# One change to a state-space and expert block: a quarter of the scans' inputs are made by ScalarE and TensorE

## The chip, the cores and the metric

The kernel runs on one NeuronCore of one Trainium2 chip. Its engines are TensorE (PE in the profile, its weight loads PEld), VectorE (DVE), ScalarE (ACT), GpSimd (POOL) and SyncE (SP, which here only issues DMAs). The metric is the time of one execution on the device in microseconds.

## The reference, cut to what matters

All data is float32. For x of shape (2, 1024, 256):

```
h  = x @ (W_base + 2 * sum_e cond[e] * B_e A_e)^T + b       # one weight per batch entry
x += mamba(h) forward + flip(mamba(flip(h)))                # two directions
x += ffn(cond2(x))                                          # 8 experts, 2 per token

mamba(h):                       # 512 channels d, 16 states n, time t
  xs, z = in_proj(h);  xs = silu(causal_conv4(xs) + cb)
  dt_r, B, C = x_proj(xs);      dt = softplus(dt_r @ W + b)
  s[d,n,t] = exp(dt[d,t] * A[d,n]) * s[d,n,t-1] + (dt[d,t] * xs[d,t]) * B[n,t]
  y[d,t]   = sum_n C[n,t] * s[d,n,t] + D[d] * xs[d,t];   out = (y * silu(z)) @ out_proj
```

The change is about the term (dt * xs) * B, the input product of a state's scan.

## The kernel before

The scans are cut into 256 units of 2 blocks of 128 channels, one state and 512 times. The four passes q (two batch entries, each forward and backward) have 64 units each: two halves of time, in each two pairs of blocks, in each the 16 states. So a group of 16 units shares its dt and its dt times x, and unit number i modulo 16 is the state. Channels lie on partitions and time along the row. The blocks of a pair are called j = 0 and j = 1.

For each unit the engines do this, every one in its own written order, held together by semaphores:

- ScalarE, `decay(i)` (L762): exp(dt * A) for both blocks. Block 1 goes into one of two PSUM banks (`DE`), block 0 into a ring of three in SBUF (`dA`). It waits until the scans two and three units before have ended.
- VectorE, `u(i)` (L964): block 0's input product, from the bank `DU` (dt times x) and a row of B, into the bank `U`. Then `scans(i)` (L974): a scan for block 1 (L988), which reads `DE` and GpSimd's product, and a scan for block 0 (L991), which reads `dA` and `U`. Results go into `hh`, a ring of three. In units 3, 7, 11, ... (every fourth, `OWN`) block 0's result stays in `U` and VectorE itself multiplies it by C (`own_product`, L994).
- GpSimd, `u(turn)` (L1218): block 1's input product for two units at a time, into `uA`. `product(i)` (L1232): the states times C for both blocks (L1245), or for block 1 alone in own units (L1241), into `hc`, a ring of four.
- TensorE, `add(i)` (L467): adds the products into two PSUM banks `Y`, as eight 128x128 transposes, so that the sum stands turned; in the last 32 units as plain products with the identity. At a group's start `turn_back`, ScalarE's copies (L801, L807) and `first_sum` (L448, D times x with a diagonal as one operand) come between. TensorE runs two units behind (`LAG`).
- SyncE, `ring_load(turn)` (L1339): the rows of B and C for two units, spread over all partitions, from DRAM into a ring of three slots, as two DMAs. A slot's load waits for GpSimd's and VectorE's last product from it.

At a group's start VectorE makes dt times x for block 0 (`du`, L954), after ScalarE has copied dt into `DU` (L778), and GpSimd for block 1 (`du`, L1209).

Beside this runs side work, placed in slots by tables at the head of the file (`STEP_AT`, `CONV_SLOTS`, `XD_AT`, `GATE_AT`, `TILE_AT` and others): the next pass's projections, convolution, step widths (softplus as Relu, Exp and Ln, added by a DMA that GpSimd issues, L1258), gates, output projection and tiles. TensorE does a unit's side work ahead of its `add`. The convolution multiplies by diagonals that ScalarE makes from the identity (`conv_diag`, L702), as it does for D (L783). Ahead of the scans stands a short stage that makes the weights and the first pass's inputs; behind them come routing and 39 expert tiles, which the change doesn't touch.

## Time and profile before

| | us |
|---|---|
| median of 3 runs | 1394.02 |
| lowest, highest | 1393.07, 1407.0 |
| the profiled execution | 1399.34 |
| its span in the trace | 1397.5 |
| the stage of the scans, in the trace | from 40 to 917 |

The profile is one execution, seen by the hardware's own recorder: every instruction with start, duration, line and what released it. Busy time counts an engine's instructions without their overlap. A wait is the engine's idle time before an instruction, put down to what ended last. Start times within an engine can be closer than the durations, since neighbouring instructions overlap by about 0.1 us. The granted clock is a share of TensorE's 2.4 GHz, and is 1.0 or 0.5 at any moment.

### The profile page before, as it was taken

The page shows a single profiled execution, that of the slowest core. Times are in us where ns is not written, and L with a number is a line of the kernel's source. Part 1 is how long each engine was busy: PE and PEld are TensorE (multiplying, and loading weights), DVE is VectorE, ACT ScalarE, POOL GpSimd, SP SyncE. Part 2 cuts the span into 40 slices and gives each one's busy share as a digit, 9 for nine tenths or more (in the row PEclk, how much of TensorE's full clock was granted, in tenths as well). Part 3 has the DMA queues.
Part 4 walks back from the last instruction along what each step waited for, and adds up shares of the span by engine and source line. Part 5 has one row for each costly group of instructions (what it writes and reads, how often), then busy time and mean ns, then how long its engine had stood idle before and what let it go on. Part 6 is the DMA issues. An engine that isn't in the chain of part 4 may idle for free.

```text
span 1397.5 us, 19024 instructions
## 1 busy us (share of the span) xinstructions
PE 1193.3 (85%) x6488; PEld 882.5 (63%) x6488; DVE 939.3 (67%) x1140; ACT 736.6 (53%) x1324; POOL 965.0 (69%) x511
## 2 busy tenths in 40 slices
PE   8878878778778768786686778898999999999997
PEld 3455544545445445455465533457999999999996
DVE  3999999999999999999999999962111111111110
ACT  4898776778785677777776574413111111111111
POOL 1999999999999999999999999921222222222211
PEclk9988889998989789798688799988999999999999
DMA  5556455555556464555466553507998999899982
GB/s 202 187 167 182 161 157 165 166 171 174 169 170 181 151 181 152 164 185 163 165 190 190 172 183 135 183 10 266 371 316 307 321 320 318 309 316 320 314 315 46
DMA packets 105507, 290.55 MB, mean 208 GB/s; under 512 B 9649, under 2 KB 19506, under 8 KB 89922
## 3 DMA queue, kind: packets, MB, share of 16 engines
q1 hardware_dynamic: 95762, 271.24, 56.0%
q0 software_dynamic: 9648, 18.09, 6.5%
q8 instruction: 52, 0.85, 0.2%
q14 instruction: 45, 0.37, 0.1%
HBM read 271.47 MB, written 9.96 MB: 201 GB/s over the span
## 4 chain that ended last, share of the span: by engine, by line
DMA 40%; PE 35%; POOL 17%; issue 3%; SPq 3%; DVE 1%; POOLq 0%; ACT 0%; DVEq 0%; ACTq 0%
DMA arena<-bc_scratch 39%; POOL arena L1245 10%; PE ps_y L653 10%; PE ps L664 9%; PE ps_u L653 5%; PE ps_du L653 5%; POOL arena L1241 4%; SPq L1349 3%; POOL arena L1229 2%; PE ps_y L368 1%; PE ps_y L442 1%; DVE arena L946 1%; PE ps_de L639 1%; PE ps_de L627 1%; DMA arena<-in_xT 0%
## 5 line engine op out<-in xcount | busy, mean ns | idle before, releaser
L1245 POOL TENSOR_TENSOR arena<-arena 128x1024 f32<-128x1024 f32 x192 | 456.6, 2404 | 16.0 <-DVE arena L991 14.3
L444 PE MATMUL ps_y<-ident,arena 128*128 128x128 f32 x1840 | 277.6, 303 | 137.1 <-POOL arena L1245 132.9
L444 PEld LDWEIGHTS ps_y<-ident,arena 128*128 128x128 f32 x1840 | 234.9, 156 | 244.8 <-POOL arena L1245 181.6
L1229 POOL TENSOR_TENSOR arena<-arena 128x1024 f32<-128x1024 f32 x127 | 303.7, 2391 | 8.4 <-issue 4.8
L773 ACT ACTIVATE ps_de<-arena,An 128x512 f32<-128x512 f32 x256 | 176.2, 688 | 203.5 <-DVE arena L988 202.6
L1294 POOL DMA_INDIRECT out_x<-arena x39 | 61.8, 1584 | 305.2 <-ACT arena L926 191.9
L972 DVE TENSOR_TENSOR ps_u<-ps_du,arena 128x512 f32<-128x512 f32 x256 | 178.7, 698 | 23.9 <-DVE arena L1002 8.6
L1196 DVE TENSOR_TENSOR arena<-ps_du,arena 128x512 f32<-128x512 f32 x39 | 27.0, 691 | 230.8 <-PE ps_du L653 227.7
L773 ACT ACTIVATE arena<-arena,An 128x512 f32<-128x512 f32 x256 | 181.3, 708 | 0.0
L988 DVE TENSOR_TENSOR_SCAN arena<-ps_de,hlast,arena 128x512 f32<-128x512 f32 x128 | 163.1, 1274 | 3.5 <-ACT arena L773 1.9
L988 DVE TENSOR_TENSOR_SCAN arena<-ps_de,arena 128x512 f32<-128x512 f32 x128 | 155.3, 1213 | 3.7 <-ACT arena L773 3.2
L653 PE MATMUL ps_y<-arena 128*128 128x128 f32 x1248 | 152.2, 275 | 2.2 <-issue 1.8
L653 PEld LDWEIGHTS ps_y<-arena 128*128 128x128 f32 x1248 | 148.4, 192 | 4.6 <-issue 1.9
L664 PE MATMUL ps<-arena 128*128 128x256 f32 x624 | 141.2, 379 | 0.5 <-issue 0.5
L664 PEld LDWEIGHTS ps<-arena 128*128 128x128 f32 x624 | 115.6, 190 | 15.0 <-issue 0.9
L991 DVE TENSOR_TENSOR_SCAN arena<-arena,hlast,ps_u 128x512 f32<-128x512 f32 x96 | 120.5, 1255 | 0.0
L350 PE MATMUL ps<-arena 128*128 128x512 f32 x224 | 114.5, 636 | 0.4 <-ACT arena L691 0.4
L991 DVE TENSOR_TENSOR_SCAN arena<-arena,ps_u 128x512 f32<-128x512 f32 x96 | 114.7, 1194 | 0.0
L926 ACT ACTIVATE arena<-ps 128x256 f32<-128x256 f32 x39 | 14.9, 383 | 180.4 <-PE ps L664 157.1
L1196 DVE TENSOR_TENSOR arena<-ps_u,arena 128x512 f32<-128x512 f32 x39 | 27.0, 691 | 120.7 <-PE ps_u L653 120.7
L920 ACT ACTIVATE arena<-ps_y 128x512 f32<-128x512 f32 x78 | 46.6, 597 | 114.0 <-PE ps_y L653 112.6
L1241 POOL TENSOR_TENSOR arena<-arena 128x512 f32<-128x512 f32 x64 | 85.0, 1328 | 0.2 <-DVE arena L988 0.2
(228 smaller groups left out, 1667.1 us busy)
## 6 DMA issues: line engine op xcount, KB each, us to landing
arena<-bc_scratch SPq DMA_DIRECT2D x256, 512.0 KB, 4.7
arena<-in_W SPq DMA_DIRECT2D x117, 1024.0 KB
arena<-arena POOLq DMA_DIRECT2D x15, 512.0 KB, 5.0
arena<-in_xT SPq DMA_DIRECT2D x2, 1024.0 KB, 6.4
arena<-in_w2c SPq DMA_DIRECT2D x1, 2048.0 KB, 8.6
arena<-in_xT SPq DMA_DIRECT2D x4, 512.0 KB, 6.1
X_scratch<-stg SPq DMA_DIRECT2D x12, 128.0 KB, 4.6
out_x<-stg SPq DMA_DIRECT2D x12, 128.0 KB, 5.0
```

Source lines behind the costliest of these rows:

```text
L350: t = e.matmul(PS[p][:, :], cdiag[:, m % 2, k, :], xp[:, m, f:f + 512], start=(k == 0), stop=(k == KC - 1))
L444: t = e.matmul(Y[j][:, part], src[:, part], ident[:, :], start=False, stop=stop, is_transpose=True, skip_group_check=True)
L653: t = e.matmul(PS[o][:, j * 128:j * 128 + 128], w[:, i % NW, k, f:f + 128], xsT[:, i % 2, k, :], start=(k == 0), stop=(k == 1))
L664: t = e.matmul(PS[7][:, 0:C], hT[:, i % 2, k, :], w2[:, i % NW, k, :], start=(k == 0), stop=(k == 7))
L773: t = e.activation(DE[i % 2][:, :] if j else dA[:, i % ND, :], dt[:, width_at(q, th, m), :], ACT.Exp, scale=An[:, q % 2, m, n:n + 1])
L972: e.tensor_tensor(U[:, :], DU[:, :], ring[:, turn % NR, 0, i % 2, :], ALU.mult).then_inc(dv_u, 1)
L988: e.tensor_tensor_scan(hh[:, i % NH, 1, :], DE[i % 2][:, :], uA[:, i // 2 % 2, i % 2, :], hlast[:, 2 * pr + 1, n:n + 1] if th else 0.0, AL ...
L991: e.tensor_tensor_scan(U[:, :] if own(i) else hh[:, i % NH, 0, :], dA[:, i % ND, :], U[:, :], hlast[:, 2 * pr, n:n + 1] if th else 0.0, AL ...
L1229: e.tensor_tensor(uA[:, turn % 2, :, :], duA.rearrange("p (o t) -> p o t", o=1).to_broadcast([128, 2, TH]), ring[:, turn % NR, 0, :, :], A ...
L1241: e.tensor_tensor(hc[:, i % NP, 1, :], hh[:, i % NH, 1, :], ring[:, turn % NR, 1, i % 2, :], ALU.mult).then_inc(gp_hc, 1)
L1245: e.tensor_tensor(hc[:, i % NP, :, :], hh[:, i % NH, :, :], c, ALU.mult).then_inc(gp_hc, 1)
L1294: e.indirect_dma_start(out, bass.IndirectOffsetOnAxis(dest[:, i:i + 1], 0), yo[:, i % 3, :], None, compute_op=ALU.add).then_inc(l_add, 16)
```

## The change

- Four states of each group, n = 6, 9, 12 and 15, are *turned units*, in all groups but the first: 60 of 256. In these, VectorE and GpSimd make no input product. Instead dt times x is transposed once a group by TensorE (`turn_inputs`) and copied to SBUF by ScalarE (`duT`, time on partitions). B's four rows are transposed likewise (`turn_rows`, `bT`). With time on partitions B[n, t] is one number a partition, so ScalarE multiplies by it with a scaled copy (`u_turned`, four of 128x256 a unit), and TensorE transposes the result back into the banks that the scans read (`u`): block 1 into `DE`, block 0 into `U`. In turned units block 1's decay goes to SBUF.
- GpSimd makes dt times x for both blocks in one instruction of 128x1024, three units ahead of the group; ScalarE copies block 0 into `DU`. In a turn with a turned unit GpSimd's input product has 128x512.
- `dA`, `uA` and `hh` become one ring `hh` of five: decays and inputs are written into it, and the scan overwrites them by the states. `hc` has three places and not four.
- The diagonals of the convolution and of D come from DRAM by SyncE's DMAs (256 KB and 128 KB each) and are no longer made by ScalarE.
- ScalarE loads one table set that holds Exp and Ln ahead of them.

```diff
-NR, ND, NH, NP, KD, LAG, EV, NW = 3, 3, 3, 4, 6, 2, 4, 3
+FLIP, STRIDE = 6, 3
+NR, NH, NP, KD, LAG, EV, NW = 3, 5, 3, 6, 2, 4, 3
...
+def flipped(i):
+    return i >= 16 and i % 16 >= FLIP and (i % 16 - FLIP) % STRIDE == 0
+DU_AT = {16 * g + 1 + j: (g, j) for g in range(1, 16) for j in range(2)}
+ROWS_AT = {max(at(q_, 32 * h_), 16 * (1 - q_ - h_)) + 3: (q_, h_) for q_ in range(NQ) for h_ in range(2)}
...
TensorE
+            def turn_inputs(i):
+                g, j = DU_AT[i]
+                e.wait_ge(gp_du, g + 1)
+                e.wait_ge(dv_sA, i - 1)
+                for part in QUARTERS:
+                    t = e.transpose(DE[i % 2][:, part], duA[:, j, part], ident[:, :])
+                t.then_inc(pe_dT, 1)
...
+            def u(i):
+                e.wait_ge(ac_uT, flips(i))
+                e.wait_ge(dv_sA, i - 1)
+                for k in range(4):
+                    t = e.transpose(DE[i % 2][:, QUARTERS[k]], uT[:, k, 128:256], ident[:, :])
+                t.then_inc(pe_u1, 1)
+                e.wait_ge(dv_sB, i)
+                if own(i - 1):
+                    e.wait_ge(dv_hc, owned(i - 1))
+                for k in range(4):
+                    t = e.transpose(U[:, QUARTERS[k]], uT[:, k, 0:128], ident[:, :])
+                t.then_inc(pe_u0, 1)
             for i in range(NU + LAG):
                 if i < NU:
                     side_work(i)
+                if i + 1 in DU_AT:
+                    turn_inputs(i + 1)
+                if i + 1 in ROWS_AT:
+                    turn_rows(i + 1)
+                if i < NU and flipped(i):
+                    u(i)
                 if i == NU:
                     out_block(1, 0, 1, both_side, (0, 1))
                 if i >= LAG:
                     add(i - LAG)
...
ScalarE
+            def logs_too():
+                if loaded[0] != "logs":
+                    e.preload_act_table_set("natural_log_exp_and_others")
+                    loaded[0] = "logs"
...
+                if i >= NH:
+                    e.wait_ge(dv_sB, i - NH + 1)
+                    e.wait_ge(gp_hc, i - NH + 1)
                 for j in (1, 0):
                     m = 2 * pr + j
-                    if j and i >= 2:
-                        e.wait_ge(dv_sA, i - 1)
-                    if not j and i >= ND:
-                        e.wait_ge(dv_sB, i - ND + 1)
-                    t = e.activation(DE[i % 2][:, :] if j else dA[:, i % ND, :], dt[:, width_at(q, th, m), :], ACT.Exp,
-                                     scale=An[:, q % 2, m, n:n + 1])
+                    to = hh[:, i % NH, j, :]
+                    if j and not flipped(i):
+                        if i >= 2:
+                            e.wait_ge(dv_sA, i - 1)
+                        to = DE[i % 2][:, :]
+                    t = e.activation(to, dt[:, width_at(q, th, m), :], ACT.Exp, scale=An[:, q % 2, m, n:n + 1])
...
+            def u_turned(i, ks):
+                q, th, pr, n = unit(i)
+                if flips(i) > 1:
+                    e.wait_ge(pe_u0, flips(i) - 1)
+                f = (n - FLIP) // STRIDE
+                for k in ks:
+                    t = e.activation(uT[:, k, :], duT[:, k, :], ACT.Copy, scale=bT[:, q % 2, th, k, f:f + 1])
+                if ks[-1] == 3:
+                    t.then_inc(ac_uT, 1)
...
+                if i + 2 < NU and flipped(i + 2):
+                    u_turned(i + 2, (0, 1))
+                if i + 1 < NU and flipped(i + 1):
+                    u_turned(i + 1, (2, 3))
...
VectorE
             def scans(i):
                 e.wait_ge(ac_dA, i + 1)
+                if flipped(i):
+                    e.wait_ge(pe_u1, flips(i))
...
+                h = hh[:, i % NH, :, :]
+                decay, x = (h[:, 1, :], DE[i % 2][:, :]) if flipped(i) else (DE[i % 2][:, :], h[:, 1, :])
+                e.tensor_tensor_scan(h[:, 1, :], decay, x, hlast[:, 2 * pr + 1, n:n + 1] if th else 0.0, ALU.mult,
+                                     ALU.add).then_inc(dv_sA, 1)
+                if flipped(i):
+                    e.wait_ge(pe_u0, flips(i))
+                else:
+                    e.wait_ge(dv_u, plain(i))
...
             for i in range(NU):
-                if i % 16 == 0:
-                    du(i)
-                u(i)
+                if i == 0:
+                    first_du()
+                if not flipped(i):
+                    u(i)
...
GpSimd
+            def du(g):
+                q, th, pr, n = unit(16 * g)
+                k = width_at(q, th, 2 * pr)
+                width_is_whole(e, 8 * q + 4 * th + 2 * pr)
+                for j in range(2):
+                    has_x(e, q, 2 * pr + j, th)
+                e.wait_ge(gp_u, 8 * g)
+                if g >= 2:
+                    e.wait_ge(pe_dT, 2 * (g - 1))
+                    e.wait_ge(ac_dc, g - 1)
+                e.tensor_tensor(duA, dt[:, k:k + 2, :], xc[q % 2][:, 2 * pr:2 * pr + 2, HB[th]], ALU.mult).then_inc(gp_du, 1)
...
             for i in range(NU):
+                if i % 16 == 13 and i + 3 < NU:
+                    du(i // 16 + 1)
...
SyncE
+            def conv_diag(q, m):
+                if m >= 2:
+                    is_full(e, ("cv", q, m - 2, 1))
+                elif q:
+                    is_full(e, ("cv", q - 1, m + 2, 1))
+                e.dma_start(cdiag[:, m % 2, :, :], d["cd"][q % 2, m]).then_inc(l_cd[m % 2], 16)
+            def sum_diag(g):
+                if g:
+                    e.wait_ge(pe_D, 2 * g)
+                e.dma_start(diag[:, :, :], d["dd"][g // 4 % 2, g % 2]).then_inc(l_D, 16)
...
+                elif i % 16 == 8 and i < NU - 16:
+                    sum_diag(i // 16 + 1)
+                if i + 1 in CONV_AT:
+                    q, m, h = CONV_AT[i + 1]
+                    if h == (q == 0) and (q or m >= 2):
+                        conv_diag(q, m)
```

## Rows read from the trace of the kernel before

**Rows 1.** Busy time of each engine from 40 to 917 us, then clock, DMA share, GB/s.
```profile
40.00:917.00 877.00, 692.17 (x3043) 432.81 (x3042) 839.81 (x949) 628.67 (x1100) 852.40 (x415) 0.87 0.53 168
```
**Rows 2.** Groups of VectorE's instructions, 40 to 917 us: busy, mean ns | idle before them.
```profile
L972 DVE TENSOR_TENSOR ps_u<-ps_du,arena 128x512 f32<-128x512 f32 x256 | 178.7, 698 | 23.9 <-DVE arena L1002 8.6 <-issue 0.4
...
L962 DVE TENSOR_TENSOR ps_du<-ps_du,arena 128x512 f32<-128x512 f32 x15 | 10.4, 690 | 0.7 <-ACT ps_du L778 0.7
```
**Rows 3.** VectorE's timeline: start us, duration us, line, shapes, idle before it.
```profile
79.14 0.68 DVE L1002 TENSOR_TENSOR arena<-ps_u,arena 128x512 f32<-128x512 f32 x1
80.02 0.70 DVE L972 TENSOR_TENSOR ps_u<-ps_du,arena 128x512 f32<-128x512 f32 x1 [0.20 <-DVE arena L1002]
80.63 1.21 DVE L988 TENSOR_TENSOR_SCAN arena<-ps_de,arena 128x512 f32<-128x512 f32 x1
81.76 1.20 DVE L991 TENSOR_TENSOR_SCAN arena<-arena,ps_u 128x512 f32<-128x512 f32 x1
83.04 0.70 DVE L972 TENSOR_TENSOR ps_u<-ps_du,arena 128x512 f32<-128x512 f32 x1
...
92.14 0.68 DVE L1002 TENSOR_TENSOR arena<-ps_u,arena 128x512 f32<-128x512 f32 x1
92.73 0.69 DVE L962 TENSOR_TENSOR ps_du<-ps_du,arena 128x512 f32<-128x512 f32 x1
93.46 0.70 DVE L972 TENSOR_TENSOR ps_u<-ps_du,arena 128x512 f32<-128x512 f32 x1
```
**Rows 4.** Groups of GpSimd's instructions, 40 to 917 us.
```profile
L1245 POOL TENSOR_TENSOR arena<-arena 128x1024 f32<-128x1024 f32 x192 | 456.6, 2404 | 16.0 <-DVE arena L991 14.3 <-DMA arena<-bc_scratch 1.4
L1229 POOL TENSOR_TENSOR arena<-arena 128x1024 f32<-128x1024 f32 x127 | 303.7, 2391 | 8.4 <-issue 4.8 <-PE ps_y L444 1.6 <-PE ps_y L442 0.4
...
L1216 POOL TENSOR_TENSOR arena<-arena 128x512 f32<-128x512 f32 x15 | 20.4, 1363 | 0.0
```
**Rows 5.** GpSimd in the timeline, from one input product to the next.
```profile
292.60 2.56 POOL L1229 TENSOR_TENSOR arena<-arena 128x1024 f32<-128x1024 f32 x1
...
298.47 2.52 POOL L1229 TENSOR_TENSOR arena<-arena 128x1024 f32<-128x1024 f32 x1
```
**Rows 6.** Ring loads, 100 to 900 us: issue ns min/median/max, then time to landing.
```profile
L1349 SPq DMA_DIRECT2D arena<-bc_scratch x234: 359/410/1098, 103.3 to 899.3; - x117
...
DMA to landing us min/median/max: 3.4/4.6/6.9
```
**Rows 7.** TensorE in the timeline: eight transposes, half a convolution, eight transposes.
```profile
297.51 1.09 PE L444 MATMUL ps_y<-ident,arena 128*128 128x128 f32 x8 [1.51 <-POOL arena L1245]
298.44 1.88 PE L350 MATMUL ps<-arena 128*128 128x512 f32 x4
...
330.29 1.97 PE L444 MATMUL ps_y<-ident,arena 128*128 128x128 f32 x8 [2.48 <-POOL arena L1245]
```
**Rows 8.** The convolution's matmuls: group with mean ns, and min/median/max ns.
```profile
L350 PE MATMUL ps<-arena 128*128 128x512 f32 x192 | 99.4, 643 | 0.0
...
L350 PE MATMUL ps<-arena x224: 590/592/1062, 69.7 to 608.2; 128*128 128x512 f32 x112
```
**Rows 9.** Groups of ScalarE's instructions, 100 to 900 us.
```profile
L773 ACT ACTIVATE ps_de<-arena,An 128x512 f32<-128x512 f32 x234 | 161.2, 689 | 193.8 <-DVE arena L988 193.0
L773 ACT ACT_TABLE_LOAD x35 | 44.9, 1283 | 0.6
L753 ACT ACT_TABLE_LOAD x14 | 18.0, 1283 | 0.2
L706 ACT ACTIVATE arena<-ident,cw 128x128 f32<-128x128 f32 x48 | 15.2, 387 | 0.0
```
**Rows 10.** The timeline at a group's start: last product, first addition, product of state 3.
```profile
311.50 1.27 POOL L1241 TENSOR_TENSOR arena<-arena 128x512 f32<-128x512 f32 x1
...
320.02 1.04 PE L444 MATMUL ps_y<-ident,arena 128*128 128x128 f32 x8
...
324.33 1.28 POOL L1241 TENSOR_TENSOR arena<-arena 128x512 f32<-128x512 f32 x1
```

## What the change was predicted to do

> **What bounds the kernel now.** I began with the busy shares of the scan stage, the 877 us in which the 256 units run [rows 1]. VectorE and GpSimd are both occupied nearly throughout (839.8 and 852.4 us), ScalarE and TensorE are not (628.7 and 692.2 us). With two engines near full, the busy share doesn't say which one sets the pace, so I read the order of VectorE's instructions next. In its timeline [rows 3] (product is L972, scans L988 and L991, own product L1002, du L962) the starts follow each other at fixed distances: product to first scan 0.61 us, first to second scan 1.13, second scan to next product 1.28, so a plain unit takes 3.02 us; in a unit whose output VectorE multiplies itself, that product and the gap behind it add 0.91. Twelve plain and four own units make some 52.0 us; sixteen such groups, with 0.12 us a unit more where scans start from stored states, du, gates and tiles, fill the stage. Its idle time before the 256 products is 23.9 us in all [rows 2], a tenth of a microsecond each, the gap behind own products and nothing more, and 16 times 52.0, with these additions, leaves no room for waits: **VectorE is the bound**. GpSimd comes next. Its idle time before its two large kinds is 16.0 and 8.4 us [rows 4], 24 us in 877, so it can follow VectorE down by some 3% and no further.
>
> **What VectorE is relieved of.** 60 of its 256 products go (states 6, 9, 12, 15 of 15 groups). 45 of them follow a plain unit: from second scan to the next first scan was 1.28 + 0.61 = 1.89, and becomes the 1.13 of two scans without a dependence: 0.76 each, 34.2 us. 15 (state 12) follow an own product: from its start to the scan was 0.88 + 0.61 = 1.49, and becomes about 0.59, the distance from own product to du [rows 3]: 0.90 each, 13.5 us. Fifteen du's go [rows 2]; each takes 0.69 us, but with it the distance from own product to next product was 1.32 against 0.88 without, so it is worth 0.44 each, 6.6 us. Together **54 us**: 877 becomes 823.
>
> **What GpSimd is relieved of.** In 60 turns the product shrinks from 128x1024 to 128x512, 2.39 to about 1.36 us [rows 4]: 61.8 us less. Its du grows from 1.36 to the 2.39 of a product of that size, 15 times: 15.5 us more. Net 46 us; busy 852.4 becomes 806, and with the 5 us that it idles on issue, 811. So 12 us of room under VectorE are left, half of what it had.
>
> **Ring loads.** Three slots are left as they are, and a load starts when GpSimd ends the last product of the turn three before. Between that and the input product that needs the slot lie one other input product and two state products: in the rows from 292.60 to 298.47, 5.87 us [rows 5]. Where the input product in that gap is a short one and one of the two is an own unit's (twice a group), the gap falls by 1.03 to 4.84 us. The load takes two issues of 0.41 and 4.6 us to land in the median, 6.9 at most [rows 6]: its second half is there after about 5.2. So GpSimd is late by 0.4 (bounds 0 and 1.5), 30 times: 12 us, of which the room of 12 hides most; I put 4 on the path (bounds 0 and 33). The diagonals of conv and D now come by 32 DMAs (6 MB) on SP's queue. Each is put behind a ring load, whose next one comes 5 us later, and their waits are for TensorE work many units old; 256 KB is a quarter of one ring turn. Nothing for these, bound 1 us each where one runs into a ring load, 32 us if all did.
>
> **TensorE's part: the new wait.** A turned unit costs 8 transposes, 1.04 to 1.09 us at full clock and 1.97 at half [rows 7]; with two times four a group for du and a few rounds for B that is 60 + 16 + 1 us, 692 to some 770 of 850. TensorE isn't the bound in the mean, but now VectorE waits for it. The second scan's input can only be turned once the scan before is over: four transposes, some 0.7 us with the signals, under the first scan of 1.13: hidden at full clock, 0.1 late at half. The first scan's input stands in TensorE's queue behind the additions of unit i-3, which wait for GpSimd's product, and behind the side work of unit i. I laid out one group. Let GpSimd start at 0 and never stop (2.34 us for 128x1024, 1.27 for 128x512: the means less the overlap of neighbours): its product 6 ends at 22.5, product 12 starts at 36.9 and ends at 39.3. VectorE's first scans of states 9, 12 and 15 begin 27.5, 36.6 and 44.9 us behind its first one of the group. Product 12 needs both scans of state 12, done 2.4 us behind the start of the first (39.0), so VectorE must have begun 2.1 before GpSimd. That puts the scan of state 9 at 25.4, 2.9 behind product 6, and that of 15 at 42.8, 3.5 behind product 12; for states 6 and 12 it is 3.3 and 3.8. So there are **2.9 to 3.8 us** from the end of product i-3 to the turned unit's first scan. The queue needs 1.1 + 0.7 + signals = 1.9 bare: enough. With a conv half or its like (1.88) it is 3.8: up to 0.9 late. Bare at half clock it is 3.3: up to 0.4 late. With such side work at half clock (3.4) 6.7: 3 to 4 late. By the slots 40 of the 60 have side work in their own unit, some 31 of that size. Conv matmuls take 643 ns in the mean, where 592 is full clock and 1062 the longest [rows 8], so 11% run at half: 3 or 4 units at 3.3, 12 us. At full clock a small lateness counts about once a group, since GpSimd catches up behind it: 15 x 0.4 = 6 us. **18 us** for TensorE; bounds 0 and 60 x 3.5 = 210.
>
> Here the Trainium skill speaks against the change: "TensorE: Matmul & The Clock Gate", Part 4 (PE-mode transpose), says that transposes don't bring the array to its full clock. By that rule more transposes give no clock back and the granted clock stays at the 0.87 of the stage or falls; rounds of eight at 1.04 us in this trace show only that they run at full clock when it is granted. The sum uses the clock as it is.
>
> **ScalarE.** 240 pieces of 128x256 with a scale: between the 0.387 us of 128x128 and the 0.689 of 128x512 [rows 9] lies 0.49, some 0.42 with the overlap of neighbours: 101 us; 30 copies of du, 16. Off go 64 conv and 32 D diagonals at about 0.32, 31 us, and with one table set for Exp and Ln the loads at L753 and as many at L773, 28 x 1.28 = 36 us. Net +50: 629 to 680 of 850. It waited 193 us for VectorE, so this is covered; only where a Silu with its two loads (3.8 us) meets two pieces (0.84) can a decay come late. 3 us; bounds 0 and 20. By the Trainium skill ("ScalarE: Activation LUTs", What ACT_TABLE_LOAD costs) a switch also drains the engine, 2.66 us in all, and 75 us would go; the rows show 0.6 us of idle before 35 loads, so the trace disagrees.
>
> **Rings.** The product ring shrinks from 4 to 3. At a group's start the last product ends at 312.8, the next group's first addition at 321.1, and product 3 starts at 324.3 [rows 10]. That product must now wait for this addition; 3 us are left, at full clock. With du's turns and half clock it fails in a few of 15 groups: 2 us (bounds 0 and 45). In three groups du's early place is 5 us behind the step widths' DMA: 1 us. The common ring of five lets decays run two units further from GpSimd; no gain, since VectorE didn't wait for it.
>
> **The sum.** 54 - 4 - 18 - 3 - 3 = 26 us. The profiled execution took 1399.3 us (span 1397.5), so 1373; the median of the three runs lies 5.3 lower, so **1368 us**.
>
> **Rivals.** (a) *The queue is never late*: leads as laid out hold, GpSimd's late loads lie in its room; VectorE's 54 us all come back: 1340. For it: TensorE idles 185 us in the stage. Against: the two late loads a group follow from plain addition. (b) *The bound passes to GpSimd through the ring*: loads land 1.2 late, 30 times, 36 us less the room of 12, and TensorE's 18: 54 - 24 - 18 - 3 - 3 = 6, or 1388, the change is hidden. For it: landings up to 6.9 us, more traffic. Against: GpSimd waited only 1.4 us for DMA in all. (c) *TensorE's queue becomes a convoy, slower than before*: the place is the first input of a turned unit. From 0.9 us of lateness per turned unit it eats the 54. If the clock is at half in those with side work, 31 x 3.5 + 20 x 0.4 = 116 us are lost: 1394 - 54 + 116 = 1456; with half of them, 1398; I take 1425. For it: TensorE already at 79%, and granted 0.87 only. Against: conv halves ran at full clock in nine cases of ten, and more work fills the gaps. The skill's rule on transposes belongs here and is part of its chance. (d) *It doesn't do what it says*, the table loads stay or a product form is slower: within the other cases' bounds, no case of its own.
>
> **Chances.** Forecast 0.52, (a) 0.15, (b) 0.18, (c) 0.15. What this kernel's measurement can tell is about 1%, 14 us. The forecast's own range, 1350 to 1384, lies nearly all in faster; (b) nearly all in same; (c) holds 0.12 slower and 0.03 same. Faster 0.67, same 0.21, slower 0.12. The range from 1338 to 1402 leaves out the worse part of (c) and the best edge of (a).
>
> **What would show it.** VectorE's product count 196 and its distance scan to scan 1.13 at turned units: step one. GpSimd's 128x1024 input products 67: step two. A VectorE wait on transposes in the first scan, its total (18 us) and whether it stands beside side work: step three. A GpSimd wait for bc_scratch before the product of turns 5 and 7 of a group: the ring. Wrong I would be if GpSimd's wait for VectorE vanished while VectorE waited for GpSimd instead, or if the granted clock of the stage moved by more than 0.05.

## The result: slower by 3.3%

| | before | after |
|---|---|---|
| median, us (4 runs each) | 1397.53 | 1442.62 |
| lowest to highest, us | 1393.07 to 1407.0 | 1437.31 to 1447.99 |
| the profiled execution, its span, us | 1399.34, 1397.5 | 1447.99, 1446.2 |
| the stage of the scans, in the trace | 40 to 917 | 40 to 965 |

The ratio is 1.033, interval [1.029, 1.0369]. 1368 us were predicted, with 1402 as the upper end: the prediction was wrong in sign, and the result lies 18 us beyond the 1425 us of rival (c).

The whole difference is in the scan stage: 925 us for 877, while what follows it takes 481 us in both. The busy time of each engine in that stage, with the columns of [rows 1]:

```profile
40.00:965.00 925.00, 752.74 (x3674) 502.49 (x3673) 794.15 (x874) 674.18 (x1252) 806.52 (x415) 0.90 0.53 166
```

VectorE's busy time fell by 45.7 us and yet the stage grew by 48, so VectorE's idle time grew from 37 to 131. Where it stands is read from the groups of VectorE's instructions (busy, mean ns | idle before them, and what ended most of it), from 40 to 965 us; `arena<-arena,hlast,ps_de` and `arena<-arena,ps_de` are the first scans of the turned units:

```profile
L1054 DVE TENSOR_TENSOR ps_u<-ps_du,arena 128x512 f32<-128x512 f32 x196 | 136.8, 698 | 21.2 <-DVE arena L1086 8.2 <-ACT ps_du L861 1.4 <-issue 0.9
L1069 DVE TENSOR_TENSOR_SCAN arena<-ps_de,hlast,arena 128x512 f32<-128x512 f32 x96 | 122.4, 1275 | 6.1 <-ACT arena L856 6.1
L1069 DVE TENSOR_TENSOR_SCAN arena<-ps_de,arena 128x512 f32<-128x512 f32 x100 | 121.5, 1215 | 15.7 <-ACT arena L856 13.1 <-POOL arena L1331 2.5
...
L1086 DVE TENSOR_TENSOR arena<-ps_u,arena 128x512 f32<-128x512 f32 x64 | 44.0, 688 | 30.2 <-PE ps_y L466 27.8 <-PE ps_y L464 1.6
L1069 DVE TENSOR_TENSOR_SCAN arena<-arena,hlast,ps_de 128x512 f32<-128x512 f32 x32 | 40.8, 1273 | 31.6 <-issue 16.4 <-PE ps_de L611 9.4 <-ACT arena L856 5.8
...
L1069 DVE TENSOR_TENSOR_SCAN arena<-arena,ps_de 128x512 f32<-128x512 f32 x28 | 33.9, 1210 | 21.3 <-PE ps_de L611 21.1
```

The same groups in the kernel before, as far as they are not in [rows 2]:

```profile
L988 DVE TENSOR_TENSOR_SCAN arena<-ps_de,hlast,arena 128x512 f32<-128x512 f32 x128 | 163.1, 1274 | 3.5 <-ACT arena L773 1.9 <-POOL arena L1229 1.4
L988 DVE TENSOR_TENSOR_SCAN arena<-ps_de,arena 128x512 f32<-128x512 f32 x128 | 155.3, 1213 | 3.7 <-ACT arena L773 3.2 <-POOL arena L1229 0.5
...
L1002 DVE TENSOR_TENSOR arena<-ps_u,arena 128x512 f32<-128x512 f32 x64 | 43.9, 687 | 1.1
```

Three waits are new: **52.9 us** before the first scans of the 60 turned units, **29.1 us** more before VectorE's own products (nearly all on the group's first addition), and **14.6 us** more before the other first scans (14.1 of them on ScalarE's decays). Take off 2.7 us less idle before the products and the 45.7 us of work saved: 52.9 + 29.1 + 14.6 - 2.7 - 45.7 = 48.2, the 48 us of the stage. The view puts 16.4 of the 52.9 us down to nothing it shows and 5.8 to ScalarE, but in the timeline 52.7 of them end with TensorE's turn of that input (L611): the scan starts within 0.25 us of its end.

GpSimd, from the same view, is not the one that holds VectorE; it waits for VectorE more than four times as long as before [rows 4]:

```profile
L1347 POOL TENSOR_TENSOR arena<-arena 128x1024 f32<-128x1024 f32 x192 | 456.1, 2387 | 70.6 <-DVE arena L1075 66.6 <-DMA arena<-bc_scratch 2.0 <-PE ps_y L466 1.9
L1331 POOL TENSOR_TENSOR arena<-arena 128x1024 f32<-128x1024 f32 x67 | 160.0, 2389 | 15.5 <-DMA arena<-bc_scratch 15.3
```

**One late turned unit.** The timeline at unit 54 (state 6). TensorE's order is: side work of a unit, the turned input if it has one, then the addition of the unit two back.

```profile
229.57 1.27 POOL L1343 TENSOR_TENSOR arena<-arena 128x512 f32<-128x512 f32 x1
...
230.90 1.92 PE L358 MATMUL ps<-arena,xpT 128*48 128x512 f32 x4
...
232.75 1.09 PE L466 MATMUL ps_y<-ident,arena 128*128 128x128 f32 x8
...
233.77 1.92 PE L358 MATMUL ps<-arena,xpT 128*48 128x512 f32 x4
234.05 1.25 DVE L1075 TENSOR_TENSOR_SCAN arena<-arena,hlast,ps_u 128x512 f32<-128x512 f32 x1
...
235.62 1.09 PE L466 MATMUL ps_y<-ident,arena 128*128 128x128 f32 x8
236.64 1.12 PE L380 MATMUL ps<-arena,dtT 16*128 16x512 f32 x2
...
237.69 0.66 PE L611 MATMUL ps_de<-ident,arena 128*128 128x128 f32 x4
238.19 0.60 PE L617 MATMUL ps_u<-ident,arena 128*128 128x128 f32 x4
238.44 1.28 DVE L1069 TENSOR_TENSOR_SCAN arena<-arena,hlast,ps_de 128x512 f32<-128x512 f32 x1 [3.14 <-issue]
```

VectorE is ready at 235.30. GpSimd's product of unit 51 ended at 230.84, 4.5 us earlier, more than the 2.9 to 3.8 us that I had laid out. But TensorE was by then still at the side work of unit 52 (230.90). Behind it stood the addition of 50, the side work of 53, the addition of 51 and the side work of 54, each running without a gap, and only then the turn, at 237.69. In this stretch it never waited, and ran at full clock: four matmuls of 128x512 in 1.92 us. It was simply two units of side work behind.

Not all late units are like this one. 30 of the 60 turned units wait over 0.3 us, 52.7 us together. I took for each the stretch from the end of GpSimd's product i-3 to the turn. In 18 of them (26.0 us) TensorE had the full clock and no idle time of half a microsecond there. In three (3.3 us) it idled for 0.5 to 1.4 us in the midst of its side work. In nine (23.4 us, all with side work of their own) its granted clock was 0.5 for a part of the stretch or all of it, and in four of the nine it idled too. The longest wait of all, at unit 220, is one of these:

```profile
836.38 2.07 PE L380 MATMUL ps<-arena,dtT 16*128 16x512 f32 x2
838.38 1.12 PE L611 MATMUL ps_de<-ident,arena 128*128 128x128 f32 x4
839.60 1.22 DVE L1069 TENSOR_TENSOR_SCAN arena<-arena,ps_de 128x512 f32<-128x512 f32 x1 [4.56 <-PE ps_de L611]
...
831.90:838.40 6.50, 6.50 (x19) 3.51 (x17) 3.07 (x7) 1.43 (x3) 5.71 (x5) 0.50 0.71 218
```

The last line is the stretch from product i-3 to the turn, with the columns of [rows 1]: TensorE busy all the time, at a granted clock of 0.50. The 51 turned units at full clock wait 29.4 us together, 0.6 each, the nine others 2.6 each.

**One group start.** The changed kernel in the timeline, at unit 160:

```profile
619.91 1.11 PE L596 MATMUL ps_de<-ident,arena 128*128 128x128 f32 x4
...
621.06 0.60 ACT L834 ACTIVATE arena<-ps_de 128x512 f32<-128x512 f32 x1 [3.85 <-PE ps_de L596]
...
623.07 1.28 DVE L1069 TENSOR_TENSOR_SCAN arena<-ps_de,hlast,arena 128x512 f32<-128x512 f32 x1 [2.55 <-ACT arena L856]
...
627.45 1.97 PE L459 MATMUL ps_y<-ident,arena 128*128 128x128 f32 x8 [2.12 <-ACT arena L888]
...
629.25 3.49 PE L483 MATMUL ps_y<-diag,arena 128*128 128x128 f32 x16
...
632.58 1.91 PE L466 MATMUL ps_y<-ident,arena 128*128 128x128 f32 x16
...
633.72 0.69 DVE L1086 TENSOR_TENSOR arena<-ps_u,arena 128x512 f32<-128x512 f32 x1 [4.31 <-PE ps_y L466]
633.78 1.29 POOL L1343 TENSOR_TENSOR arena<-arena 128x512 f32<-128x512 f32 x1 [5.05 <-PE ps_y L466]
...
619.00:631.00 12.00, 9.88 (x36) 6.74 (x35) 7.04 (x7) 6.57 (x12) 9.73 (x5) 0.50 0.49 165
```

ScalarE stands 3.85 us behind TensorE's turn of dt times x, with the decays behind it, so VectorE's scan is 2.55 us late. ScalarE's copies that `turn_back` needs come late too, the group's first addition starts at 632.58, and only it frees the product place that state 3 needs: VectorE's own product waits 4.31 us and GpSimd's 5.05. By the last line TensorE had a granted clock of 0.50 from 619 to 631 us, so this group, the worst of the 15 for the own product, is late by order and by clock together.

### The profile page after: what moved, and what is told of

Same layout as the page of the kernel before. It is cut to its first block and busy times, and to the rows that moved or that the text cites. A ratio compares the mean times of both kernels' runs of the same rounds, so it can differ in the third digit from the quotient of the medians.

```text
span 1446.2 us, 20708 instructions
## 1 busy us (share of the span) xinstructions
PE 1255.5 (87%) x7120; PEld 952.5 (66%) x7120; DVE 895.3 (62%) x1065; ACT 782.6 (54%) x1477; POOL 919.8 (64%) x511
## 5 line engine op out<-in xcount | busy, mean ns | idle before, releaser
L1347 POOL TENSOR_TENSOR arena<-arena 128x1024 f32<-128x1024 f32 x192 | 456.1, 2387 | 70.6 <-DVE arena L1075 66.6
L466 PE MATMUL ps_y<-ident,arena 128*128 128x128 f32 x1840 | 263.1, 294 | 58.3 <-POOL arena L1347 57.8
L466 PEld LDWEIGHTS ps_y<-ident,arena 128*128 128x128 f32 x1840 | 228.1, 152 | 121.9 <-POOL arena L1347 81.9
L856 ACT ACTIVATE arena<-arena,An 128x512 f32<-128x512 f32 x316 | 218.4, 710 | 0.1
L856 ACT ACTIVATE ps_de<-arena,An 128x512 f32<-128x512 f32 x196 | 134.7, 687 | 93.5 <-DVE arena L1069 85.0
L1331 POOL TENSOR_TENSOR arena<-arena 128x1024 f32<-128x1024 f32 x67 | 160.0, 2389 | 15.5 <-DMA arena<-bc_scratch 15.3
L1054 DVE TENSOR_TENSOR ps_u<-ps_du,arena 128x512 f32<-128x512 f32 x196 | 136.8, 698 | 21.2 <-DVE arena L1086 8.2
L869 ACT ACTIVATE arena<-arena 128x256 f32<-128x256 f32 x240 | 108.0, 498 | 61.8 <-PE ps_u L617 61.7
L1069 DVE TENSOR_TENSOR_SCAN arena<-ps_de,arena 128x512 f32<-128x512 f32 x100 | 121.5, 1215 | 15.7 <-ACT arena L856 13.1
L1069 DVE TENSOR_TENSOR_SCAN arena<-ps_de,hlast,arena 128x512 f32<-128x512 f32 x96 | 122.4, 1275 | 6.1 <-ACT arena L856 6.1
```

The costliest lines, as they stand in the source:

```text
L466: t = e.matmul(Y[j][:, part], src[:, part], ident[:, :], start=False, stop=stop, is_transpose=True, skip_group_check=True)
L856: t = e.activation(to, dt[:, width_at(q, th, m), :], ACT.Exp, scale=An[:, q % 2, m, n:n + 1])
L869: t = e.activation(uT[:, k, :], duT[:, k, :], ACT.Copy, scale=bT[:, q % 2, th, k, f:f + 1])
L1054: e.tensor_tensor(U[:, :], DU[:, :], ring[:, turn % NR, 0, i % 2, :], ALU.mult).then_inc(dv_u, 1)
L1069: e.tensor_tensor_scan(h[:, 1, :], decay, x, hlast[:, 2 * pr + 1, n:n + 1] if th else 0.0, ALU.mult, ALU.add).then_inc(dv_sA, 1)
L1331: e.tensor_tensor(to, duA[:, 1:2, :].to_broadcast([128, 2, TH]), ring[:, turn % NR, 0, :, :], ALU.mult).then_inc(gp_u, 1)
```

## The experiments

Ratios are to the kernel before, timed beside it on the same chip, with 95% intervals. "Gained" is against the changed kernel's ratio of 1.033.

**Theory (T):** TensorE's queue is late by its order. A turned unit's input stands behind side work and additions, and every lateness is passed on by ScalarE and the group's first addition. **Rivals:** the third product place (R1), ring and du edits without the turned units (R2), the scaled copies on ScalarE (R3), the amount of TensorE's work, whatever its order (R4).

Rows in this section are of the groups of VectorE's instructions in the scan stage, unless another view is named.

### b_np3: the third product place alone, in the kernel before

```diff
-NR, ND, NH, NP, KD, LAG, EV, NW = 3, 3, 3, 4, 6, 2, 4, 3
+NR, ND, NH, NP, KD, LAG, EV, NW = 3, 3, 3, 3, 6, 2, 4, 3
```

> The kernel before with the product ring hc cut from four places to three, nothing else. Theory A (the small ring is one of the two costs): VectorE's own product of state 3 must now wait for the group's first addition, some 2 us in each of 15 groups, so 20 to 35 us slower than before, about 1422. Theory B (only the turned units cost): the ring hides as I predicted, at most 3 us, about 1397.

1408.19 us, ratio 1.0058 [1.0036, 1.0081]. VectorE's own products wait 14.5 us, 11.3 of them for the first addition:

```profile
L1002 DVE TENSOR_TENSOR arena<-ps_u,arena 128x512 f32<-128x512 f32 x64 | 44.0, 687 | 14.5 <-PE ps_y L444 11.3 <-PE ps_y L442 2.1
```

So the place costs 8 us by itself, between my two expectations (20 to 35, and at most 3), four times the 2 us of my sum, and is no explanation of 45.

### noflip: the change without its turned units

```diff
 def flipped(i):
-    return i >= 16 and i % 16 >= FLIP and (i % 16 - FLIP) % STRIDE == 0
+    return False
-DU_AT = {16 * g + 1 + j: (g, j) for g in range(1, 16) for j in range(2)}
+DU_AT = {}
...
+ROWS_AT = {}
```

> The changed kernel with no turned unit at all: VectorE and GpSimd make all 256 input products, everything else (common ring, three products, diagonals by DMA, GpSimd's double du, one table set) as changed. Theory A: VectorE is relieved of 7 us of du but waits 30 us at state 3: 1410 to 1425. If only turned units cost: 1390. If the new common ring or the DMAs cost too: over 1430.

1404.55 us, ratio 1.0068 [1.004, 1.0097], less than the 1410 to 1425 that I expected. The own products wait longer than in b_np3:

```profile
L1085 DVE TENSOR_TENSOR arena<-ps_u,arena 128x512 f32<-128x512 f32 x64 | 44.0, 687 | 21.6 <-PE ps_y L466 20.1 <-PE ps_y L464 0.5
```

R2 is bounded: ring, wide du, DMA'd diagonals, fewer table loads and the third product place cost 9 us together. That is a net sum: in the profiled execution the scans take from 40 to 929 us, 12 longer than before, VectorE is busy 8.5 us less in them, and idle 20 us more, all of it before the own products. The turned units, which were to bring the gain, cost the other 38 us.

### own2: VectorE's own unit one state earlier

```diff
-OWN = (3, 7, 11, 15, 19, 23, 27, 31)
+OWN = (2, 7, 11, 15, 18, 23, 27, 31)
```

> The changed kernel with the own unit at state 3 moved to state 2, whose product needs an addition of the group before. Theory A: VectorE's wait before its own products (30 us) falls under 5 us and the time by 15 to 30 us, to about 1420; part comes back as waits at the turned units of state 6. Theory B (TensorE is simply overloaded, a wait removed shows up elsewhere): within 8 us of the changed kernel's 1443.

1439.74 us, ratio 1.0294 [1.0258, 1.0331], 5 us gained, as the second of the two expectations had it. The waits before own products are gone, 30.2 to 1.1 us, but those before the turned units' first scans grew by 20, from 53 to 73 us:

```profile
L1086 DVE TENSOR_TENSOR arena<-ps_u,arena 128x512 f32<-128x512 f32 x64 | 43.9, 687 | 1.1
L1069 DVE TENSOR_TENSOR_SCAN arena<-arena,hlast,ps_de 128x512 f32<-128x512 f32 x32 | 40.7, 1273 | 40.3 <-issue 22.6 <-ACT arena L856 8.9 <-PE ps_de L611 8.7
L1069 DVE TENSOR_TENSOR_SCAN arena<-arena,ps_de 128x512 f32<-128x512 f32 x28 | 33.9, 1211 | 32.5 <-PE ps_de L611 31.7 <-ACT arena L856 0.9
```

R1 falls as a cause of its own in the changed kernel: VectorE meets TensorE's backlog at state 3 or at state 6, and a wait that is removed at one comes back at the other.

### early and first: the turned inputs forward in TensorE's order

```diff
-                t.then_inc(pe_u1, 1)
+                t.then_inc(pe_u1, 1)
+
+            def u_second(i):
                 e.wait_ge(dv_sB, i)
...
             for i in range(NU + LAG):
+                if i < NU and flipped(i):
+                    u_second(i)
                 if i < NU:
                     side_work(i)
...
-                if i < NU and flipped(i):
-                    u(i)
+                if i + 1 < NU and flipped(i + 1):
+                    u(i + 1)
```

This is first; in early, `u_second(i)` stands where `u(i)` stood, behind the side work.

> The changed kernel, but TensorE turns the first scan's input a unit earlier, ahead of the additions of unit i-3 and of the side work of unit i; the second input stays behind the side work. Theory A (the first input's place in the queue is the other cost): of the 53 us that VectorE waits before turned units' first scans most goes; 20 to 40 us faster than the changed kernel, about 1412; some waits pass to the second scan. Theory B (TensorE lacks time, not order): within 8 us of 1443.

> The changed kernel with both turned inputs ahead of the unit's side work: the first also ahead of the additions of unit i-3, the second right behind the second scan of unit i-1. The kernel with the first alone moved took 14 us off; between the two kernels with late turns the second took another 20. If both are costs of place in the queue: 30 to 40 us under 1443, about 1408. If TensorE lacks time: above 1420.

early: 1428.83 us, ratio 1.0195 [1.0144, 1.0246]. first: 1423.6 us, ratio 1.0191 [1.0151, 1.0231]. Both gained 19 us by their ratios, so the second step, which took 27 us of waits away, gained nothing that can be told from noise. Both missed what I expected (about 1412 and 1408), and first lies in the range that I had given to TensorE lacking time (above 1420). In early the first scans of the turned units wait 4.7 us instead of 52.9, but their second scans now wait 33, since the second input is still behind the side work. In first, whose rows follow, these waits are 6 us:

```profile
L1079 DVE TENSOR_TENSOR_SCAN arena<-arena,hlast,ps_u 128x512 f32<-128x512 f32 x93 | 117.0, 1258 | 2.9 <-PE ps_u L619 2.8
L1079 DVE TENSOR_TENSOR_SCAN arena<-arena,ps_u 128x512 f32<-128x512 f32 x96 | 114.8, 1196 | 1.7 <-PE ps_u L619 1.7
L1090 DVE TENSOR_TENSOR arena<-ps_u,arena 128x512 f32<-128x512 f32 x63 | 43.3, 688 | 34.1 <-PE ps_y L466 30.1 <-PE ps_y L464 3.2
...
L1079 DVE TENSOR_TENSOR_SCAN ps_u<-arena,ps_u 128x512 f32<-128x512 f32 x32 | 38.6, 1207 | 1.4 <-PE ps_u L619 1.3
L1073 DVE TENSOR_TENSOR_SCAN arena<-arena,hlast,ps_de 128x512 f32<-128x512 f32 x30 | 38.0, 1267 | 4.5 <-ACT arena L860 3.2 <-issue 1.2
L1073 DVE TENSOR_TENSOR_SCAN arena<-arena,ps_de 128x512 f32<-128x512 f32 x28 | 33.7, 1203 | 4.4 <-PE ps_de L611 4.2
```

T holds for the waits, and in time for less than half of the loss: 44 us of waits before first scans went, 6 came up before second scans, and the time fell by 19. The rest of the lateness is now paid at the group start (34.1 us before own products, 34.4 us in all before the plain first scans). And TensorE now stands still ahead of side work and additions: it waits 45.8 us for VectorE before it turns second inputs, where it waited 38.9 in the changed kernel, and 13.7 us for ScalarE's scaled copies, where it waited 0.7.

### late, early_late, first_late, early_late_np: the turns two units later

```diff
-DU_AT = {16 * g + 1 + j: (g, j) for g in range(1, 16) for j in range(2)}
+DU_AT = {16 * g + 3 + j: (g, j) for g in range(1, 16) for j in range(2)}
```

and B's rows two units sooner.

> The changed kernel with the turning of dt times x two units later (states 3 and 4 of the group in place of 1 and 2) and that of B at state 1 in place of 3. Theory A (the group's start costs because ScalarE waits in its own order for TensorE's turns just before it must copy Y): ScalarE's wait for the du transposes (56 us) falls under 35, VectorE's wait before own products (30 us) to about 15, 10 to 20 us faster than the changed kernel, about 1428. Theory B (three product places are the cost, wherever the turns stand): within 6 us of 1443.

> Both edits: the first input turned ahead of the additions, and du turned two units later. Theory A: the savings add up (14 us and 10 to 20), about 1413. Theory B: like the early one alone, 1425 to 1430.

> As the kernel with both edits, and the second input turned ahead of the unit's side work too, so that no turned input stands behind side work. If side work in front is what is left of the queue's cost: the 33 us that VectorE waits before turned units' second scans nearly go, and the time falls by 10 to 25 us more, to about 1395. If TensorE lacks time: the side work, held back by the wait for the second scan, comes late, and nothing or less is gained, 1410 or more.

> As the kernel with both edits, with four product places and four places in the common ring (the same memory) in place of three and five. If the product ring holds back the group's start: the wait before own products goes, 10 to 20 us less than with both edits, about 1398. If it only moves to the turned unit of state 6, as when the own unit was shifted: within 5 us.

All four came out slower than I had expected (1395 to 1428 us), and the fourth product place changed nothing, as its second expectation had it. 1489.43 us, ratio 1.0665 [1.0612, 1.0719], for late; 1.0609 [1.0554, 1.0663] for early_late; 1.047 [1.0409, 1.053] for first_late; 1.0639 [1.0589, 1.0689] with four product places and a ring of four beside it. I had put the turns at a time when I took TensorE for idle; in late's timeline one of the two now stands behind `first_sum` (L483):

```profile
229.14 3.78 PE L483 MATMUL ps_y<-diag,arena 128*128 128x128 f32 x16
...
236.00 0.66 PE L596 MATMUL ps_de<-ident,arena 128*128 128x128 f32 x4
...
236.69 0.60 ACT L834 ACTIVATE arena<-ps_de 128x512 f32<-128x512 f32 x1 [6.74 <-PE ps_de L596]
```

The miss tells more than the hits: the same instructions, at other places in the order, cost 47 us. R4 can't be all: the amount of TensorE's work is the same in both.

### soon, first_soon, first_soon_np: the turns a unit sooner

```diff
-DU_AT = {16 * g + 1 + j: (g, j) for g in range(1, 16) for j in range(2)}
+DU_AT = {16 * g + j: (g, j) for g in range(1, 16) for j in range(2)}
```

B's rows are turned one unit sooner too, and ScalarE's turned copy waits for its own last scaled pieces.

> The changed kernel with the turning of dt times x one unit earlier (states 0 and 1 of the group in place of 1 and 2) and that of B at state 2. Two units later cost 46 us, because the second turn stood in TensorE's queue behind the group's first sums. Theory A (at the group's start TensorE and ScalarE wait for each other in turn, and the turns must be done before the sums are copied): ScalarE's wait for these transposes falls under 40 us and the time by 5 to 20, about 1430. Theory B (its place at 1 and 2 is ahead of the sums already, nothing left to win): within 5 us of 1443.

> Both: turned inputs ahead of the side work, and du turned one unit earlier. Theory A: 1443 - 35 - 13 = 1395, with 20 us or more still lost before own products of state 3. Theory B: as the kernel with the inputs alone, about 1408.

> The same with four product places and four common ones in place of three and five. If what is left is the wait of own products for the group's first addition: 10 to 20 us less, about 1380, faster than before. If it passes on to the turned unit of state 6, or the common ring of four binds: within 5 us of the kernel with three.

soon: 1429.39 us, ratio 1.0236 [1.0162, 1.0309]. first_soon: 1414.92 us, 1.0136 [1.0105, 1.0167]. With four product places and a ring of four: 1.013 [1.0087, 1.0173]. So the two edits, 19 and 13 us alone, gain 27 together, and the fourth place gains nothing, though the own products' wait falls from 17.2 to 1.1 us. I had expected 1395 to 1408 and, with the fourth place, either 1380 or no more than 5 us. In first_soon a single wait is left that is larger than 20 us, and it has a new place:

```profile
L1060 DVE TENSOR_TENSOR ps_u<-ps_du,arena 128x512 f32<-128x512 f32 x196 | 136.8, 698 | 48.4 <-ACT ps_du L867 31.1 <-DVE arena L1092 5.8 <-issue 0.9
```

ScalarE's copy of dt times x into VectorE's bank needs nothing from TensorE, but stands in ScalarE's order behind a copy that waits for TensorE's turn (66.4 us in 19 waits, up to 9.0).

### copy_first, copy_turn_first, copy_turn_first_np, scaled_last: the rest, step by step

```diff
                 logs_too()
+                if n == 0 and i:
+                    e.wait_ge(gp_du, i // 16 + 1)
+                    e.wait_ge(dv_u, plain(i - 1))
+                    e.activation(DU[:, :], duA[:, 0, :], ACT.Copy).then_inc(ac_dc, 1)
                 if i in DU_AT:
...
             for i in range(NU + LAG):
                 if i < NU and flipped(i):
                     u_second(i)
+                if i + 1 in DU_AT:
+                    turn_inputs(i + 1)
+                if i + 1 in ROWS_AT:
+                    turn_rows(i + 1)
                 if i < NU:
                     side_work(i)
...
-NR, NH, NP, KD, LAG, EV, NW = 3, 5, 3, 6, 2, 4, 3
+NR, NH, NP, KD, LAG, EV, NW = 3, 4, 4, 6, 2, 4, 3
```

and in scaled_last `u_turned` at the end of ScalarE's step. Each piece is moved, not doubled: the copy is gone from behind the decays, and the turns from behind the side work.

> first_soon (second input ahead of the side work, next unit's first input ahead of the addition, turns of dt times x one unit sooner) with ScalarE's copy of dt times x into VectorE's bank put ahead of the turned copies. Theory (ScalarE's order at the group start is what is left): VectorE's 31 us of waits before its product (L1060, <- ACT L867) go below 5, and the time falls by 20 to 30 us, to 0.995 +- 0.006 of before. Rival (VectorE is held elsewhere anyway, by GpSimd or by TensorE's first addition at the same place): the wait moves to the own product or the first scan and the time falls by less than 8 us.

> copy_first, and TensorE's turns of dt times x and B stand ahead of its side work too. Theory: ScalarE's wait for the turns (66 us in 19 waits in first_soon) falls below 35 and decays are no longer late at group starts; 5 to 10 us less than copy_first. Rival: ScalarE's waits were covered, within 3 us of copy_first; or the first addition of the group and with it the own product comes later.

> copy_turn_first with four product places and four places in the common ring. Theory: the own product's wait for the first addition (17 us in first_soon) goes, 5 to 10 us less than copy_turn_first, 0.985 of before. Rival (the ring of four holds ScalarE's decays back by as much, as first_soon_np against first_soon showed 1 us): within 3 us of copy_turn_first.

> copy_turn_first_np with ScalarE's scaled pieces of dt times x behind its side work of the same step and no longer ahead of it. Theory (their wait for the second input of the turned unit before, 46 us in 39 waits, holds the decays): VectorE's wait for decays goes from 19 to below 8 and the time falls by 5 to 10 us, 0.993 of before: the first version faster than before. Rival (the pieces then come late after a Silu with its table loads, and the turned unit's first scan waits for them): 0 to 10 us slower, with the first scans' waits above 30 us.

| | median us | ratio |
|---|---|---|
| copy_first | 1407.63 | 1.0064 [1.004, 1.0089] |
| copy_turn_first | 1402.18 | 1.0028 [1.0003, 1.0054] |
| copy_turn_first_np | 1397.49 | 0.9999 [0.9975, 1.0022] |
| scaled_last | 1392.5 | 0.997 [0.9941, 0.9999] |

Moving one copy ahead of another took 31.1 us of waits away (0.5 left) and returned 10 us, not the 20 to 30 that I expected: 17 us came back before the plain first scans (14 to 31), 3 before own products. The next two steps gave 5 and 4 us, where 5 to 10 each were expected; copy_turn_first_np was to reach 0.985. In scaled_last VectorE's wait for decays is 14.4 us and not below 8; it is faster than before by 4 to 5 us of 1398, an effect at the edge of its interval. The last version's rows:

```profile
L1060 DVE TENSOR_TENSOR ps_u<-ps_du,arena 128x512 f32<-128x512 f32 x196 | 136.8, 698 | 20.0 <-DVE arena L1092 8.4 <-issue 0.9
L1075 DVE TENSOR_TENSOR_SCAN arena<-ps_de,hlast,arena 128x512 f32<-128x512 f32 x96 | 122.4, 1275 | 9.0 <-ACT arena L866 5.5 <-POOL arena L1337 3.6
L1075 DVE TENSOR_TENSOR_SCAN arena<-ps_de,arena 128x512 f32<-128x512 f32 x100 | 121.4, 1214 | 12.7 <-ACT arena L866 7.7 <-POOL arena L1337 4.5
...
L1092 DVE TENSOR_TENSOR arena<-ps_u,arena 128x512 f32<-128x512 f32 x64 | 43.9, 686 | 1.1
L1075 DVE TENSOR_TENSOR_SCAN arena<-arena,hlast,ps_de 128x512 f32<-128x512 f32 x32 | 40.5, 1267 | 12.4 <-issue 11.3 <-ACT arena L866 1.2
...
L1075 DVE TENSOR_TENSOR_SCAN arena<-arena,ps_de 128x512 f32<-128x512 f32 x28 | 33.8, 1207 | 9.6 <-PE ps_de L611 9.3
```

What is left is 44 us before first scans, where the kernel before has 7. The view puts it down to ScalarE (14.4), TensorE (9.3), GpSimd (8.1) and, 11.3 us, to none; in the timeline those 11.3 end with TensorE's turns too. Another 8 stand before second scans. These 44 us more are about what the removed products saved. The 4 to 5 us are not gained in the scan stage at all: in the profiled executions the last scan ends at 918.3 us, before at 916.9; it is what follows that took 475 us for 481, at a granted clock of 0.99 there for 0.97. No edit touches that part, and in the profiled executions of all 20 kernels here it took 472 to 476 us in seven and 479 to 487 in thirteen, whatever the order of the scans. So it is shown that the edits brought the 45 us back, and not that this version is faster than the kernel before.

### group_start_only: the same group start, turned inputs left behind

> The changed kernel with the group start of copy_turn_first (turns of dt times x one unit sooner and ahead of TensorE's side work, ScalarE's copy into VectorE's bank ahead of the turned copies), but both inputs of a turned unit still behind the side work and with the addition order unchanged. If the two places add up: copy_turn_first is 43 us under the changed kernel and moving the inputs alone (first) was worth 19, so this is worth 24, a ratio of 1.016 +- 0.004, with VectorE's waits in the turned units' first scans still 50 us or more. Rival (the turned units are the convoy and everything else follows from them): less than 12 us gained, ratio above 1.024. Other rival (the group start alone sets off the lateness of the units behind it): the first scans' waits fall below 30 us and the ratio is below 1.010.

1435.07 us, ratio 1.0276 [1.0236, 1.0316], 8 us gained. Of the three expectations it is the rival in which everything follows from the turned units (less than 12 us gained). The turned units' first scans still wait 65 us (36.4 and 28.4), read from an execution 10 us faster than the median. The same edits of copy and turns are worth 15 us on top of first_soon (1.0136 to 1.0028) and nothing on top of soon (1.0236 to 1.0276, the intervals overlap). So the two places don't add up; the turned inputs behind the side work are the first cause.

### plain_np: noflip with four product places and a ring of four

> noflip (all of the change but the turned units) with four product places and four places in the common ring. Theory: noflip's 9 us are the third product place, as in b_np3, so this comes within 3 us of before. Rival (du by one wide GpSimd product, the DMA diagonals or ScalarE's copy of dt times x cost them): 5 us or more stay.

1422.42 us, ratio 1.0156 [1.0105, 1.0208]; I had expected about the time of before. The own products' wait is gone (1.1 us), but the ring of four now holds GpSimd: its input product of a later unit needs a place that its own state product must free first, and it idles 18.8 us, in 111 waits of up to 0.2 us, for the end of that product.

```profile
L1068 DVE TENSOR_TENSOR_SCAN arena<-ps_de,hlast,arena 128x512 f32<-128x512 f32 x128 | 163.2, 1275 | 13.9 <-POOL arena L1329 10.2 <-ACT arena L855 1.9 <-issue 1.7
L1068 DVE TENSOR_TENSOR_SCAN arena<-ps_de,arena 128x512 f32<-128x512 f32 x128 | 155.6, 1216 | 18.9 <-POOL arena L1329 13.9 <-ACT arena L855 4.2
```

That 24 us of waits for GpSimd appear only here, where it has no turned units to relieve it: four places in the common ring are enough with them (copy_turn_first_np gained 4 us) and too few without. I had taken the ring's size for free in both.

## Why the prediction was wrong, step by step

- **What bounds the kernel: right.** VectorE had no waits worth naming, and its new waits of 97 us, less the work saved, explain the whole stage.
- **VectorE relieved of 54 us: right in kind, and spent in full.** The count is 196 as predicted. Its busy time fell by 45.7 us, and its idle time before products and du's by 3.4; where the other 5 of the 54 went the views don't show.
- **GpSimd: right.** 806 us busy were predicted, 806.5 measured. In no kernel with turned units was it the one that set the pace, so rival (b) falls.
- **Ring loads: right.** GpSimd's large input products wait 15.3 us for them (12 predicted), in 18 waits, and VectorE waits 2.5 us for these products, where I put 4 on the path.
- **TensorE's turned inputs: the step that failed.** "So there are 2.9 to 3.8 us from the end of product i-3 to the turned unit's first scan. The queue needs [...] 1.9 bare". The lead was there (4.5 us at unit 54), but the queue wasn't empty at its start. I added up the side work of unit i alone and took TensorE to have caught up with GpSimd at unit i-3. The side work of units i-1 and i-2 stood there too. Counted by the tables of slots, the 16 turned units with side work in their own unit and in both before it wait 1.67 us each, the 29 with side work in two of the three 0.78, and the 15 others 0.23. The term is 53 us where I put 18, 0.88 us a unit. That is rival (c)'s point of decision, 0.9, from two causes. The larger is a backlog at full clock: 29.4 us, where I had 6. The other is the one that rival (c) named, half clock in units with side work: 23.4 us in nine units, where I had 12 in three or four. I had read the share of half clock off the convolution's matmuls, 11%; the stage's granted clock of 0.87 [rows 1] is a quarter of the time. One wait I put at nothing: TensorE stands 38.9 us before its turns of the second inputs, for VectorE's second scan and own product, with the additions behind it. The 185 us that TensorE idles in the stage are an average; they are no reserve in a row of units that each bring 1.9 us of side work and 1.1 us of addition to the 3.1 us of a unit.
- **The product ring: wrong by place.** I priced its loss at GpSimd's product of state 3, with 3 us of slack, and overlooked that VectorE's own product of the same state takes a place too and comes earlier. 29 us more of waits, where "rings" had 3. Without any turned unit it is 13 us (b_np3, 8 us of time) and 20 (noflip), so at most a third of it needs the turned units. Half clock is no exception here, as I had it: in b_np3, 10.7 of the 13.6 us stand in the five groups whose granted clock from the first scan to the own product was below 0.7; in the kernel before, three groups are so low.
- **ScalarE: the work right, the order wrong.** 680 us busy were predicted, 674 measured. But I costed only its durations. Three of its new instructions wait for TensorE (61.7 us in `u_turned`, 56.2 in the turned copy of dt times x, 5.7 in that of B), and a decay behind them comes late: 14.1 us where I put 3. Before, its only long wait was for VectorE, 203 us, which is cover; of that 85 are left.
- **Rival (c), 0.15, priced 1425:** right in place and sign, 18 us short. Its half clock is under half of the wait at its place, and it had nothing for the last two points.

By the Trainium skill ("Perfetto Trace Analysis", Tensor Engine Instruction (MATMUL, LD_WEIGHTS)), ScalarE, VectorE and GpSimd take their instructions strictly in order; the traces agree: in first_soon a copy whose data were ready came late behind one that waited, and with the two exchanged its wait fell from 31.1 to 0.5 us.

What stays open: whether the remaining 44 us can go with a place for the turns that isn't shared with the decays (a further PSUM bank), or with a fourth product place beside a ring of five; neither was built. How much is TensorE's amount of work rather than its order is open too: no kernel here has the same order with less work. So is what half clock costs by itself, since no run changed the clock alone, and R3: no kernel with turned units does without the scaled copies. In the changed kernel TensorE's turns wait 0.7 us for them, in scaled_last 11.4, so they were not the first cause and are a part of what is left.

## What to carry to other kernels

Work moved to an engine that idles a fifth of the time is hidden only if that engine is idle at the moment at which the bound engine needs the result. Walk its queue back over several units with their side work until it is empty, rather than from the last hand-over, and walk it at both levels of the clock where the granted clock of the stage is under 1. On an engine in the middle, list which of its new instructions wait and what stands behind each: here one copy in the wrong place was worth 10 us. And where removing a wait moves it to the next hand-over, the waits have one source upstream; mending it in order along the chain gave 50 us back, mending the last link alone 5 to 8.

## What was not expected of the hardware

**The granted clock rose with more transposes.** noflip and the changed kernel differ in the turned units alone, on TensorE only transposes (480 for the inputs, 120 for dt times x, 32 for B). The row of noflip's stage:

```profile
40.00:929.00 889.00, 706.78 (x3041) 442.27 (x3040) 831.32 (x934) 566.47 (x974) 867.83 (x415) 0.85 0.55 173
```

The clock stands at 0.85 without them and at 0.90 with them, and the kernel before had 0.87 [rows 1]. The Trainium skill ("TensorE: Matmul & The Clock Gate", Part 4) says that transposes don't bring the array to its full clock; by that rule the clock would have stayed or fallen. These two runs don't agree with it. They don't show why the clock rose: the turns fill gaps between other work too.

**Table loads cost their duration.** One set for Exp and Ln took 80 loads down to 52, 28 as predicted, at 1283 ns each with 0.5 us of idle before 26 of them.
